# Decay of the first two token tiles by two sigmoids instead of two tanh and an affine step, with the gelu table loaded behind them

## The reference, cut to what matters

```python
# block 1: gated linear recurrence ("attention")
q = silu(x @ Wq1 @ Wq2)
f = sigmoid(x @ Wk1 @ Wk2)
log_f = log_sigmoid(f)
a = exp(log_f)                 # that is, a = sigmoid(sigmoid(x @ Wk1 @ Wk2))
k = 1.0 - a
v = x @ Wv
h[i] = a[i] * h[i-1] + k[i] * v[i]      # associative scan over the 512 tokens
out = q * h
out = out * rsqrt(mean(out * out) + 1e-6) * norm_w
return out @ Wo
# block 2: six feed-forward blocks
x = gelu(x @ W1[i].T + B1[i]) @ W2[i].T + B2[i] + x
x = layernorm(x) * LN_G[i] + LN_B[i]    # not after the last
```

## Time and profile before

| | |
|---|---|
| median of the runs | 634.91 us |
| the profiled execution | 635.04 us |
| its span (first to last instruction) | 633.0 us |
| TensorE matmul busy | 621.2 us, 98% |
| VectorE busy | 464.6 us, 73% |
| ScalarE busy | 411.3 us, 65%, 686 instructions |
| GpSimd busy | 252.7 us, 40% |
| granted TensorE clock | 1.0, full speed over the whole span |

### The profile page before, as it was taken

The page is one execution under the profiler, slowest core; times in us unless marked ns, Lnnn a source line. Parts: engine busy times, 40 slices in busy tenths (PEclk is TensorE's granted clock), DMA queues, the critical chain, the costliest instruction groups (busy, mean ns, idle before and its releaser), DMA issues.

```text
span 633.0 us, 9056 instructions
## 1 busy us (share of the span) xinstructions
PE 621.2 (98%) x2913; PEld 517.6 (82%) x2913; DVE 464.6 (73%) x809; ACT 411.3 (65%) x686; POOL 252.7 (40%) x234
## 2 busy tenths in 40 slices
PE   8998999999999999999999999999999999999996
PEld 6787888888788888888888888888888888888886
DVE  5998857877666876776797678767767976786565
ACT  5999985867856665665566466656655664556454
POOL 5684411428534354135352243541353522213033
PEclk9999999999999999999999999999999999999999
DMA  8210000002211020011110110200111100003522
GB/s 289 67 35 1 2 2 0 2 10 74 59 38 23 19 71 6 3 37 38 39 35 5 40 24 16 71 7 4 36 39 38 37 5 6 5 4 72 121 75 67
DMA packets 51599, 24.10 MB, mean 38 GB/s; under 512 B 43104, under 2 KB 47584, under 8 KB 51552
## 3 DMA queue, kind: packets, MB, share of 16 engines
q1 hardware_dynamic: 51264, 23.26, 14.1%
q10 hardware_dynamic: 288, 0.26, 0.1%
HBM read 19.51 MB, written 4.00 MB: 37 GB/s over the span
## 4 chain that ended last, share of the span: by engine, by line
PE 90%; ACT 3%; DVE 3%; issue 2%; POOL 1%; DMA 0%; POOLq 0%; DVEq 0%; ACTq 0%
PE BK L497 45%; PE BK L807 39%; PE BK L608 2%; PE BK L817 1%; ACT R L395 1%; PE BK L452 1%; POOL X L635 1%; PE BK L621 0%; DMA X<-in_x 0%; PE BK L471 0%; ACT OH L595 0%; DVE XL L701 0%; ACT SB L597 0%; ACT WH L351 0%; DVE HL L799 0%
## 5 line engine op out<-in xcount | busy, mean ns | idle before, releaser
L793 ACT ACTIVATE HH<-BK,B 128x512 fp32r<-128x512 f32 x192 | 132.2, 688 | 176.1 <-PE BK L497 174.7
L799 DVE TENSOR_TENSOR HL<-BK,HH 128x512 fp32r<-128x512 f32 x192 | 130.4, 683 | 98.0 <-ACT BK L796 96.1
L497 PE MATMUL BK<-XH,WL 128*128 128x512 f32 x416 | 162.5, 391 | 0.9 <-DVE XL L484 0.7
L497 PE MATMUL BK<-XH,WH 128*128 128x512 f32 x416 | 162.1, 390 | 0.0
L497 PE MATMUL BK<-XL,WH 128*128 128x512 f32 x416 | 162.0, 389 | 0.0
L807 PE MATMUL BK<-HH,WL 128*128 128x512 f32 x368 | 143.6, 390 | 0.0
L807 PE MATMUL BK<-HH,WH 128*128 128x512 f32 x368 | 143.3, 389 | 0.0
L807 PE MATMUL BK<-HL,WH 128*128 128x512 f32 x368 | 143.2, 389 | 0.0
L796 ACT ACTIVATE BK<-BK,B 128x512 f32<-128x512 f32 x192 | 125.5, 653 | 0.0
L497 PEld LDWEIGHTS BK<-XH,WL 128*128 128x128 f32 x416 | 78.1, 188 | 17.4 <-DVE XL L484 0.9
L687 POOL TENSOR_TENSOR RN<-VN,MH 128x16 f32<-128x16 f32 x20 | 58.2, 2911 | 84.4 <-DVE VN L685 84.4
(11 more groups left out here) (131 smaller groups left out, 786.2 us busy)
## 6 DMA issues: line engine op xcount, KB each, us to landing
STG<-in_w SPq DMA_DIRECT2D x24, 512.0 KB, 3.8
G<-sums SPq DMA_DIRECT2D x160, 8.0 KB, 1.7
out<-R SPq DMA_DIRECT2D x16, 128.0 KB, 1.9
X<-in_x SPq DMA_DIRECT2D x3, 512.0 KB, 7.6
R<-turns SPq DMA_DIRECT2D x3, 512.0 KB, 4.0
sums<-P SPq DMA_DIRECT2D x40, 8.0 KB, 1.4
R<-in_wv SPq DMA_DIRECT2D x1, 512.0 KB, 5.6
STG<-in_wo SPq DMA_DIRECT2D x1, 512.0 KB, 6.0
```

Source lines behind the costliest of these rows:

```text
L497: r = e.matmul(dst, s, m, start=first and i == 0, stop=last and i == len(todo) - 1)
L793: lambda e, ev=ev, hs=hs, bias=bias: e.activation(HH[:, hs, :], bank_of[ev][:, :], ACT.Gelu, bias=bias),
L799: lambda e, ev=ev, hs=hs: e.tensor_tensor(HL[:, hs, :], bank_of[ev][:, :], HH[:, hs, :].bitcast(f32), ALU.subtract), ("hlo", n, j))
```

## The change

For t = 0 and 1 the decay is made by two instructions: Sigmoid of the bank into FB ("t1"), and Sigmoid of FB into AB ("a"), which waits for the scan that last used this AB buffer. The product kv then is (AB - 1) * v instead of (KB - 1) * v. As KB - 1 is twice a - 1, the scan's result is half of what it was for these two tiles, and the epsilon that `L629` adds to the mean square goes from 16 to 4 times. Tiles 2 and 3 keep the three instructions. The first ScalarE instruction becomes a Sigmoid, and a new Gelu on one column ("gelu_in") is planned behind the last sigmoid of tile 1, with a planned duration of 1.6 us; the first real Gelu is ordered behind it.

```diff
-         ... "warm": 2.9, "idle_in": 0.53, ...
+         ... "warm": 2.9, "gelu_in": 1.6, "idle_in": 0.53, ...
...
-        op("scalar", -96.5, [("one",)], lambda e: e.activation(WARM[:, :], ONE[:, :], ACT.Gelu), ("warm",))
+        op("scalar", -96.5, [("one",)], lambda e: e.activation(WARM[:, :], ONE[:, :], ACT.Sigmoid), ("warm",))
+        op("scalar", A_AT[1] + A_LONG[1] - 4, [("after", ("a", 1, 3)), ("one",)],
+           lambda e: e.activation(WARM[:, :], ONE[:, :], ACT.Gelu), ("gelu_in",))
...
+                last = "a" if i <= 8 else "t2"
+                if t < 2:
+                    op("scalar", M + 1.0, [zk, *before(last, 1)],
+                       lambda e, zk=zk: e.activation(FB[:, :], bank_of[zk][:, :], ACT.Sigmoid), ("t1", t, m))
+                    op("scalar", M + 1.7, [("t1", t, m), *before("scan")],
+                       lambda e, ab=ab: e.activation(ab, FB[:, :], ACT.Sigmoid), ("a", t, m))
+                else:
+                    ...    # the three instructions of before
-                op("vector", M + 3.3, [v, ("t2", t, m)],
-                   lambda e, kb=kb, v=v: e.scalar_tensor_tensor(bank_of[v][:, :], kb, -1.0, bank_of[v][:, :],
+                op("vector", M + 3.3, [v, ("a" if t < 2 else "t2", t, m)],
+                   lambda e, kb=ab if t < 2 else kb, v=v: e.scalar_tensor_tensor(bank_of[v][:, :], kb, -1.0, bank_of[v][:, :],
...
-               ... EPS_LN / 512, 16 * EPS_RMS * EPS_LN,
+               ... EPS_LN / 512, (4 if t < 2 else 16) * EPS_RMS * EPS_LN,
...
-                op("scalar", K + 1.5, [("mm1", n, j), *at("mm2", HR), ("ldb1",)],
+                op("scalar", K + 1.5, [("mm1", n, j), *at("mm2", HR), ("ldb1",), *([("after", ("gelu_in",))] if n + j == 0 else [])],
```

More of the change, by code:

```diff
@@ L40 @@
          "ft": 0.38, "pre": 0.4, "end": 0.52, "part": 0.52, "z_vs": 0.2, "z_ng": 0.2, "z_ct": 0.47, "z_rs": 0.55, "eps": 0.1, "fin0": 0.41, "fin1": 0.75,
-         "mhalf": 0.1, "quarter": 0.1, "half": 0.1, "one": 0.06, "warm": 2.9, "idle_in": 0.53, "spin": 5.3, "up_a": 0.39, "up_z": 0.39, "up_b": 0.39, "up_c": 0.39, "up_d": 0.39, "up_e": 0.39}
+         "mhalf": 0.1, "quarter": 0.1, "half": 0.1, "one": 0.06, "warm": 2.9, "gelu_in": 1.6, "idle_in": 0.53, "spin": 5.3, "up_a": 0.39, "up_z": 0.39, "up_b": 0.39, "up_c": 0.39, "up_d": 0.39, "up_e": 0.39}
 FREE = {"sync": 0.0, "scalar": 0.11, "vector": 0.09, "gpsimd": 0.05, "tensor": 0.16}
@@ L577, in sandwich @@
                 ab, kb, qb, hb = AB[:, p, :], KB[:, p, :], QB[:, m, :], SB[:, m, :]
[L580 to L585, removed]
-                op("vector", M + 3.3, [v, ("t2", t, m)],
-                   lambda e, kb=kb, v=v: e.scalar_tensor_tensor(bank_of[v][:, :], kb, -1.0, bank_of[v][:, :],
+                last = "a" if i <= 8 else "t2"
[5 more added lines that the diff above has]
+                else:
+                    op("scalar", M + 1.0, [zk, *before(last, 1)],
+                       lambda e, zk=zk: e.activation(FB[:, :], bank_of[zk][:, :], ACT.Tanh, scale=0.5), ("t1", t, m))
+                    op("scalar", M + 1.7, [("t1", t, m), ("quarter",), *before("kv"), *before("a")],
+                       lambda e, kb=kb: e.activation(kb, FB[:, :], ACT.Tanh, scale=0.25, bias=QU[:, :]), ("t2", t, m))
+                    op("scalar", M + 2.4, [("t2", t, m), ("half",), *before("scan")],
+                       lambda e, ab=ab, kb=kb: e.activation(ab, kb, ACT.Identity, scale=0.5, bias=HALF[:, :]), ("a", t, m))
+                op("vector", M + 3.3, [v, ("a" if t < 2 else "t2", t, m)],
+                   lambda e, kb=ab if t < 2 else kb, v=v: e.scalar_tensor_tensor(bank_of[v][:, :], kb, -1.0, bank_of[v][:, :],
                                                                 ALU.add, ALU.mult), ("kv", t, m))
@@ L628, in sandwich @@
             op("vector", Z + 0.3, [("rms", t)],
-               lambda e, t=t: e.tensor_scalar(MS[:, t, :], bank_of["rms", t][:, 0:4], EPS_LN / 512, 16 * EPS_RMS * EPS_LN,
+               lambda e, t=t: e.tensor_scalar(MS[:, t, :], bank_of["rms", t][:, 0:4], EPS_LN / 512, (4 if t < 2 else 16) * EPS_RMS * EPS_LN,
                                               ALU.mult, ALU.add), ("ms", t))
```

## The result

The changed kernel took 635.93 us (median of 20 runs) against 634.90 us for the kernel before: the ratio is 1.0024, with a 95% interval of 1.0015 to 1.0032. It became slower by about 1 us, where I had forecast 2 us faster. One of the 20 runs took 3582.68 us, and the profile of that set was taken in it, so the profile shown here is that of the same kernel run once more (635.61 us, span 633.8 us; 635.84 us median of 12 runs, ratio 1.0022, 1.0013 to 1.0030).

A forecast was written before the change was run, and what follows sets the result against it. TensorE's work and its gaps between 20 and 60 us were taken as the bound. Gains of 0.5 and 2.3 us less 0.8 us for the load made 2.0 us, giving 632.9 us, range 630.6 to 636.3.

The forecast's parts named there:

- The bound: TensorE's work plus its gaps sets the time; closing the gaps in 20 to 60 us gains at most about 4.6 us.
- The sum for ScalarE: Before the first Gelu, ScalarE has 5.0 + 0.8 - 1.5 = 4.3 us less work.
- The load: Second table load and one-column Gelu, behind tile 1's last sigmoid: 1.5 us on ScalarE, 0.8 us charged to the time.
- The scan: Tile 0's third-group scan on VectorE no longer waits for the affine step: at about 23.8 us, 3.3 us earlier.
- The step that failed: Path from tile 0's fourth group through norms and transposes to block 2's first mm1 ends some 2 to 3 us earlier.
- the 2.3 us of gaps: TensorE's gaps from 50 to 60 us: the shorter path to block 2 fills 2.3 of 2.6 us.
- the sum: Total gain in time: 0.5 + 2.3 - 0.8 = 2.0 us.
- rival 2: Load and new order cost more than they give, before TensorE's needs at 51 to 57 us: 636.4 us; chance 0.19.
- The half microsecond at 26.00 us: TensorE's 1.22 us gap before 26.00 us shrinks by 0.5 us, one square less standing between the four copies.
- Rival 1: VectorE's queue from 20 to 50 us sets TensorE's gaps: within 0.5 us of before, 634.9 us; chance 0.23.

The follow-up runs named there:

- Rms_early: The changed kernel with the planner keys of tile 0's last projection and of its sum of squares 5 us lower: 639.28 us, ratio 1.0078.
- old_order: The two-sigmoid instructions put into the order planned for the kernel before, second load where the last affine step stood: 634.34 us, ratio 0.9993.
- norm_first: The changed kernel with tile 2's l1 copies planned 8 us earlier and its transposes 3 us earlier: 634.77 us, ratio 1.0001.
- same_order_no_load: The changed kernel's order with Tanh for both sigmoids of tiles 0 and 1 and the gelu table from the start, no second load: 635.98 us.

## Why the prediction was wrong

*The bound* held. TensorE's gaps between 20 and 60 us decided the time, and hardly anything behind them moved. Its size was off: I scaled the four waits that are reported to 4.6 us, while by starts about 6.4 us were lost there.

*The sum for ScalarE* was near. Eight affine steps went; the second function takes 633 ns, 0.09 us less than 727 (forecast 0.10); the load takes what the one of before took. Lines of ScalarE in the changed kernel, first 60 us:

```profile
L587 ACT ACTIVATE AB<-FB 128x512 f32<-128x512 f32 x8 | 5.1, 633 | 0.1
...
L304 ACT ACT_TABLE_LOAD x1 | 1.3, 1283 | 0.0
```

Busy time fell by 3.6 us (411.3 to 407.7), where I had 4.3.

*The load* stood where I put it, and it shows no drain. ScalarE's timeline, changed kernel:

```profile
50.13 0.64 ACT L587 ACTIVATE AB<-FB 128x512 f32<-128x512 f32 x1
50.79 1.28 ACT L304 ACT_TABLE_LOAD   x1
52.09 0.20 ACT L304 ACTIVATE WARM<-ONE 128x1 f32<-128x1 f32 x1
52.20 0.61 ACT L604 ACTIVATE OH<-QB 128x512 fp32r<-128x512 f32 x1
```

From the end of the last sigmoid (50.77) to the next useful instruction are 1.43 us, load and one-column Gelu included. The 2.66 us of the Trainium skill (ScalarE: Activation LUTs, What ACT_TABLE_LOAD costs) are not seen, though ScalarE came straight from work. The 0.8 us that I charged to TensorE's path are 0: without the load the same order takes as long (635.98 against 635.84 us).

*The scan* came when forecast: 23.66 us (I said 23.8), from 27.08. The fourth group's first function starts at 21.84 us instead of 28.26 and its second at 27.23 instead of 29.68, 6.4 and 2.5 us earlier where I had said 2. The fourth scan is 1.7 us earlier (31.17 against 32.83 us).

*The step that failed* is "Behind the fourth group of tile 0 hangs the whole path to block 2 ... I expect this path to end some 2 to 3 us earlier", and with it the 2.3 us of gaps that this path was to fill. It took an advance of ScalarE's part for one of the whole path. The sum of squares on TensorE kept 0.2 us of the advance (39.90 against 40.08 us), the second norm's last step on GpSimd came 0.8 us later than before (46.08 against 45.28), and the transposes of the third norm 0.9 us later, at 56.24 us. Their row in the kernel before:

```profile
55.37 1.06 PE L471 MATMUL BK<-ID,R 128*128 128x128 f32 x8
```

On the path stand queues that run in order. Rms_early showed that TensorE's held the advance first, and that the other three lose it again behind. The first mm1 comes at 60.82 us instead of 59.04, but of these 1.8 us only about 0.8 is lateness: one more projection of tile 1 (12 matmuls, 1.4 us) stands ahead of it and two matmuls of the narrow products fewer (0.5 us). So instead of filling 2.3 us of the gaps from 50 to 60 us, TensorE was idle there for 2.00 us instead of 2.24, and for 1.21 us more in 40 to 50 us.

*What I left out of the sum* is the order. I named it in rival 2, as an addition to the load's price with no number. It was the whole loss: +1.5 us for the new order (old_order against the changed kernel), against about -0.6 us for the instructions. Most of it is one place, the transposes and narrow products of tile 2 behind tile 1's projections: norm_first moves them and gives back 1.1 us. The other 0.4 us was not traced to a place.

*The half microsecond at 26.00 us* did not come. The square has gone from between the four copies, as I said, and the transposes start 0.4 us earlier (25.58), but TensorE's work in front of them ends 0.5 us earlier too, and the wait is 1.17 us where it was 1.06. Right behind it stands a new wait of 1.38 us, for the low part at 26.37 us that runs into GpSimd's second subtraction. It looks like the cause and isn't: the changed kernel is ahead at 46.80 us, and norm_first keeps both waits.

Rival 2 had the right sign and, at 636.4 us, about the right size, by the wrong mechanism: its price was the load, which costs nothing, and its condition was not met (the last sigmoid of tile 1 starts at 50.13 us, the second tanh in its place before at 51.59). That 635.93 us lies inside my range is luck of the same kind. Rival 1 is open in part: ScalarE does show gaps now and VectorE is at 10.00 of ten in 30 to 40 us, but no run relieved VectorE alone.

*Still open:* why the planner's orders differ so much is shown only by their results, not derived from its rules; where the last 0.4 us of the order's cost arise; and no order was found that turns ScalarE's free time into more than 0.6 us.

## What to carry to other kernels

When a planner fixes the order, count a removed instruction twice: by its duration, and by the new order it brings. Replay the old order with the new instructions, as old_order does, before judging the instructions; here the two effects had opposite signs, and neighbouring inputs spread from 634 to 642 us. An advance on one engine reaches the end only if every in-order queue on the path has room for it; follow the path through each queue and ask what stands in front there. And before blaming the longest new wait, compare the two kernels at a place where the bounding engine has done the same work: only what is late there is lost.

## What the runs showed of the hardware

The clock. A long wait of TensorE can cost more than itself. In same_order_no_load, after the waits of 1.12 and 1.38 us at 25.55 and 27.99 us, the profiled execution has a granted clock of 0.83 from 25 to 35 us, and matmuls of 128x512 start 0.42 us apart at 30.92 and 31.34 us, where 0.23 is usual:

```profile
25.00:30.00 5.00, 3.07 (x18) 2.87 (x19) 4.39 (x8) 4.81 (x9) 4.72 (x4) 0.83 0.27 83
```

The later wait that ends at 48.39 us in the changed kernel ends at 49.95 us there, 1.6 us later. That execution took 637.28 us where the median is 635.98. The same waits in the profiled execution of the changed kernel came with a clock of 1.00. So the same gap sometimes lowers the clock and sometimes not: beside the one long run, 5 of the other 19 runs of the changed kernel took 637.3 to 640.4 us, with a mean granted clock of 0.992 to 0.997 where the others have 0.998 or more, while the 55 runs of the kernel before beside these and beside the repeat, whose early gaps are shorter, all stayed under 635.5 us.

The long run. In the run of 3582.68 us every matmul was slow for the whole execution, 1.70 us on average instead of 0.39, with 1.00 in the records of the granted clock. Part 5 of its page:

```profile
L499 PE MATMUL BK<-XH,WL 128*128 128x512 f32 x416 | 707.2, 1700 | 0.0
```

The other engines' instructions kept their durations (the Gelu 688 ns). It happened once, and what it was stays open.
